# Two value stretches of eight heads instead of four of four, in the second layer's attention of a one-core kernel

## The reference

```python
qh = (q @ Wq).reshape(B, N, 16, 64).transpose(0, 2, 1, 3)
kh = (kv @ Wk).reshape(B, M, 16, 64).transpose(0, 2, 1, 3)
vh = (kv @ Wv).reshape(B, M, 16, 64).transpose(0, 2, 1, 3)
attn = softmax(einsum('bhnd,bhmd->bhnm', qh, kh) / 8)
out = einsum('bhnm,bhmd->bhnd', attn, vh)      # the "attention values"
x = x + tanh(g) * (out.reshape(B, N, 1024) @ Wo + bo)
# then layernorm, router (top 8 of 64), a shared expert, and the routed experts
```

## Time and profile before

| what | value |
|---|---|
| time, median of 3 runs | 2510.68 us (2510.32 to 2510.93) |
| span of the profiled execution | 2514.6 us |
| PE busy | 2403.0 us (96%) |
| PEld busy | 1805.6 us (72%) |
| ACT busy | 1612.6 us (64%) |
| DVE busy | 1597.9 us (64%) |
| POOL busy | 731.2 us (29%) |

### The profile page before, as it was taken

How to read it: one execution, slowest core, us unless ns; L and a number is a source line. 1 busy time by engine, 2 the same in 40 slices (tenths; PEclk the granted TensorE clock), 3 DMA queues, 4 the chain that set the end, 5 groups by cost and what they waited for, 6 DMA issues and landing times. The chain is left out here.

```text
span 2514.6 us, 63718 instructions
## 1 busy us (share of the span) xinstructions
PE 2403.0 (96%) x19932; PEld 1805.6 (72%) x19933; DVE 1597.9 (64%) x5004; ACT 1612.6 (64%) x4909; POOL 731.2 (29%) x871
## 2 busy tenths in 40 slices
PE   7999999999998899999999999999999967999997
PEld 5777777777777566666666666666666657888885
DVE  4777777777774466676776776776776753433338
ACT  3777777777774466666666666666666626777770
POOL 2000000000000022232233232233233245777771
PEclk7999999999999999999999999999999989999998
DMA  5111111111110501111111111111111257666679
GB/s 158 34 48 46 39 47 46 39 47 46 39 42 13 158 28 39 39 43 40 38 42 41 37 42 40 38 43 42 36 42 43 59 151 242 198 192 192 194 261 379
DMA packets 145291, 210.10 MB, mean 84 GB/s; under 512 B 23976, under 2 KB 108506, under 8 KB 145026
## 3 DMA queue, kind: packets, MB, share of 16 engines
q1 hardware_dynamic: 114322, 139.92, 19.0%
q0 software_dynamic: 26544, 60.21, 7.2%
q10 hardware_dynamic: 4160, 6.55, 0.7%
HBM read 118.21 MB, written 96.75 MB: 85 GB/s over the span
## 5 line engine op out<-in xcount | busy, mean ns | idle before, releaser
L1455 ACT ACTIVATE wup<-bank,nmax 112x375 f32<-112x375 f32 x512 | 297.2, 586 | 111.9 <-DVE nmax L1559 110.7
L767 ACT ACTIVATE prob<-bank,nmax 112x375 f32<-112x375 f32 x512 | 294.1, 587 | 54.9 <-DVE nmax L851 51.0
L851 DVE TENSOR_REDUCE nmax<-bank 112x1 f32<-112x375 f32 x512 | 254.9, 540 | 88.7 <-PE bank L589 88.7
L1903 POOL DMA_INDIRECT expert_rows<-rows,ids x248 | 237.2, 957 | 154.4 <-ACT wup L1455 107.3
L1559 DVE TENSOR_REDUCE nmax<-bank 112x1 f32<-112x375 f32 x512 | 255.5, 541 | 21.1 <-PE bank L1251 21.1
L1314 PE MATMUL bank<-wup,wk 128*128 128x375 f32 x512 | 219.9, 512 | 1.9 <-DMA wup<-context_turned 0.8
L1020 POOL TENSOR_TENSOR stats<-stats,neg_half 112x1 f32<-112x1 f32 x64 | 35.1, 549 | 632.3 <-DVE stats L881 628.3
L1461 ACT COPY pT<-bank 128x336 f32<-128x336 f32 x512 | 201.5, 451 | 19.3 <-PE bank L1258 19.1
L596 PE MATMUL bank<-ident,prob 112*128 112x112 f32 x1536 | 200.0, 263 | 7.6 <-ACT pT L773 1.7
L1870 POOL TENSOR_TENSOR stats<-stats,neg_half 112x1 f32<-112x1 f32 x64 | 35.6, 557 | 566.2 <-DVE stats L1590 564.0
L1251 PE MATMUL bank<-wup 64*112 64x375 f32 x1024 | 195.9, 501 | 3.3 <-ACT wup L1455 3.3
(11 more groups left out here) (284 smaller groups left out, 5321.4 us busy)
## 6 DMA issues: line engine op xcount, KB each, us to landing
xr<-expert_rows SPq DMA_DIRECT2D x274, 129.0 KB
wup<-expert_results SPq DMA_DIRECT2D x14, 1024.0 KB, 18.2
wdn<-expert_results SPq DMA_DIRECT2D x14, 1024.0 KB, 20.8
wdn<-in_L_ffn_W_down_dram SPq DMA_DIRECT2D x8, 1024.0 KB, 12.6
expert_rows<-nowhere SPq DMA_DIRECT2D x56, 129.0 KB, 2.9
x_and_h_in<-stage SPq DMA_DIRECT2D x32, 224.0 KB, 2.4
xt<-x_and_h_in SPq DMA_DIRECT2D x32, 224.0 KB, 2.8
context_turned<-ctxT SPq DMA_DIRECT2D x32, 187.5 KB, 2.2
```

Source lines behind the costliest of these rows:

```text
L767: nc.scalar.activation(prob[:, n % RING, :NK], s_bank[r][:NQ, :NK], ACT.Exp, bias=nmax[:, r:r + 1], accum_out=rsum[:, par, h:h + 1]).then_ ...
L851: nc.vector.tensor_reduce(nmax[:, r:r + 1], s_bank[r][:NQ, :NK], AX, ALU.max, negate=True).then_inc(maxed, 1)
L1455: nc.scalar.activation(prob[:, n % RING, :NK], s_bank[r][:NQ, :NK], ACT.Exp, bias=nmax[:, r:r + 1], accum_out=rsum[:, par, n:n + 1]).then_ ...
L1903: nc.gpsimd.indirect_dma_start(rows_d, bass.IndirectOffsetOnAxis(ap=ids[:, k:k + 1], axis=0), rows[:, k, :], None).then_inc(scattered, 16)
```

## The change

The values of a sequence are made in two stretches of eight heads (va0, va1) instead of four of four. Each of them now stands directly behind a group's scores on PE. The inverted sums follow: two reciprocals, two widened copies of 8 x 64 columns, two groups of four transposes, two copies to `rT`, two normalising multiplications, each over twice the columns. The ring of turned probabilities has 12 places instead of 8. `rexp`, `rT` and `xT` are laid into the space of a weight buffer that is free in this stage (`wup`), `x1ln` into a bias tile, and tanh works in place. The copy of lnT goes from DVE to ACT. The order list is laid anew: v11, lnT move to the act lane, k4 and k7 to the dve lane, and most slots change.

```diff
 ORDER_C = [
-    (1, "post", "va3", "dve"), (1, "own", "v10", "act"), (1, "own", "v11", "dve"),
-    (2, "own", "r0", "act"), (2, "post", "wo", "dve"), (3, "own", "v12", "act"), (3, "pre", "k2", "dve"),
-    (5, "pre", "k4", "act"), (5, "post", "lnT", "dve"), (6, "pre", "k1", "act"), (6, "pre", "xT", "dve"),
-    (7, "own", "va0", "dve"), (8, "pre", "k0", "act"), (8, "post", "router", "dve"), (9, "post", "shared_up", "act"),
-    (9, "pre", "k3", "dve"), (9, "own", "r1", "act"), (10, "pre", "k5", "act"), (10, "own", "va1", "dve"),
-    (10, "own", "r2", "act"), (12, "pre", "q0", "act"), (12, "pre", "v00", "dve"), (12, "pre", "v01", "act"),
-    (13, "post", "rank", "dve"), (13, "own", "r3", "act"), (14, "post", "shared_down", "dve"),
-    (14, "pre", "v02", "act"), (15, "pre", "k6", "dve"), (15, "pre", "q1", "act"), (15, "own", "va2", "dve"),
-    (15, "pre", "k7", "act"),
+    (1, "post", "va1", "dve"), (1, "own", "v10", "act"), (2, "own", "v11", "act"), (2, "post", "wo", "dve"),
+    (3, "own", "v12", "act"), (5, "pre", "k2", "dve"), (5, "post", "lnT", "act"), (6, "pre", "k4", "dve"),
+    (6, "pre", "k1", "act"), (6, "pre", "xT", "dve"), (7, "own", "r0", "act"), (7, "post", "router", "dve"), (7, "pre", "k0", "act"),
+    (8, "pre", "k3", "dve"), (8, "post", "shared_up", "act"),
+    (9, "own", "va0", "dve"), (9, "pre", "q0", "act"), (10, "pre", "k5", "act"), (11, "pre", "v00", "dve"),
+    (12, "pre", "v01", "act"), (13, "post", "rank", "dve"), (13, "pre", "v02", "act"), (14, "post", "shared_down", "dve"),
+    (14, "pre", "q1", "act"), (15, "pre", "k6", "dve"), (15, "own", "r1", "act"), (15, "pre", "k7", "dve"),
 ]
...
-    PT_RING = 8
+    PT_RING = 12
+    NG = 2
+    PER = H // NG
...
-                        freed(pe, i, later(*(f"v{g // 2}{c}" for c in range(KC))))
-                        wait_kept(pe, i, 4 * g + 4)
-                        for a in range(2):
+                        all_freed(pe, i, *(f"v{g}{c}" for c in range(KC)))
+                        wait_kept(pe, i, PER * (g + 1))
+                        for a in range(PER // 2):
...
                 def router(p, par, n):
                     misc = lane("router", n)
+                    other_lane("router", p, "lnT")
...
+                def keep_lnT(p, par, n):
+                    misc = full(act, "act", n)
+                    nc.scalar.copy(flat(x1T[:]), misc[:, :CC * NQ]).then_inc(lane_free["act"], 1)
...
-                    dve.wait_ge(exped, H * i + 4 * g + 4)
+                    dve.wait_ge(exped, H * i + PER * (g + 1))
...
-                    nc.vector.tensor_copy(rexp[:, g % 2, :].rearrange("q (h d) -> q h d", d=DK),
-                                          rinv[:, heads].unsqueeze(2).to_broadcast([NQ, 4, DK])).then_inc(expanded, 1)
+                    nc.vector.tensor_copy(rexp.rearrange("q (h d) -> q h d", d=DK),
+                                          rinv[:, heads].unsqueeze(2).to_broadcast([NQ, PER, DK])).then_inc(expanded, 1)
...
                 def inverses(i, par, n):
-                    for v, at in enumerate((0, 7, 8, 12)):
+                    for v, at in enumerate((4, 12)):
                         if n == at:
                             inverse(i, par, v)
...
-                sp.wait_ge(lane_full["dve"], uses.out(NB - 1, "va3"))
+                freed(sp, NB - 1, "va1")
                 experts_up(3)
```

More of the change, by code:

```diff
@@ L1091, in later @@
         return max(names, key=place)
-    for one, other in ([("xT", "q0"), ("xT", "q1"), ("va3", "wo"), ("wo", "lnT"), ("lnT", "router"), ("lnT", "shared_up"),
-                        ("router", "rank"), ("shared_up", "shared_down"), ("va0", "va1"), ("va1", "va2"), ("r0", "r1"), ("r1", "r2")]):
+    for one, other in ([("xT", "q0"), ("xT", "q1"), ("va1", "wo"), ("wo", "lnT"), ("lnT", "router"), ("lnT", "shared_up"),
+                        ("router", "rank"), ("shared_up", "shared_down"), ("r0", "va0")]):
         assert place(one) < place(other)
@@ L1331, in f @@
                         misc = lane(f"r{g}", n)
-                        pe.wait_ge(expanded, NT * p + g + 1)
-                        for a in range(2):
-                            mm = pe.transpose(misc[:, a * NQ:(a + 1) * NQ], rexp[:, g % 2, a * P:(a + 1) * P], ident[:NQ, :NQ])
+                        pe.wait_ge(expanded, NG * p + g + 1)
+                        for a in range(PER // 2):
+                            mm = pe.transpose(misc[:, a * NQ:(a + 1) * NQ], rexp[:, a * P:(a + 1) * P], ident[:NQ, :NQ])
                         left(mm, f"r{g}")
@@ L1374, in _ @@
                 hooks |= {f"q{g}": q(g) for g in range(2)} | {f"k{p}": k(p) for p in range(PAIRS)}
-                hooks |= {f"v{half}{c}": v(half, c) for half in range(2) for c in range(KC)} | {f"r{g}": inverse(g) for g in range(NT)}
-                hooks |= {f"va{g}": values(g) for g in range(NT)}
+                hooks |= {f"v{half}{c}": v(half, c) for half in range(2) for c in range(KC)} | {f"r{g}": inverse(g) for g in range(NG)}
+                hooks |= {f"va{g}": values(g) for g in range(NG)}
                 for _ in range(20):
@@ L1439, in room_in_pT @@
             def room_in_pT(eng, i, n):
-                g = n // 4 - PT_RING // 4
-                valued(eng, i if g >= 0 else i - 1, g % NT)
+                last = H * i + n - PT_RING
+                valued(eng, last // H, last % H // PER)
             def room_in_vals(eng, j, half):
-                valued(eng, j - 1, 2 * half + 1)
+                valued(eng, j - 1, half)
             @block.scalar
@@ L1452, in exponentials @@
                     if n == 0:
-                        wait(act, inverted, NT * (i - 1))
+                        wait(act, inverted, NG * (i - 1))
                     wait(act, turned, H * i + n + 1 - RING)
@@ L1460, in keep_turned @@
                     room_in_pT(act, i, n)
-                    nc.scalar.copy(pT[:, n % PT_RING, :], pt_bank[n % 2][:, :KC * NQ]).then_inc(kept_act, 1)
+                    nc.scalar.copy(pT[:, (H * i + n) % PT_RING, :], pt_bank[n % 2][:, :KC * NQ]).then_inc(kept_act, 1)
                 def q(g):
@@ L1488, in f @@
                         misc = full(act, "act", n)
-                        freed(act, p if g >= 2 else p - 1, f"va{(g - 2) % NT}")
-                        nc.scalar.copy(rT[:, g % 2, :], misc[:, :2 * NQ]).then_inc(lane_free["act"], 1)
-                    return f
+                        freed(act, p if g else p - 1, f"va{1 - g}")
+                        nc.scalar.copy(rT[:], misc[:, :PER // 2 * NQ]).then_inc(lane_free["act"], 1)
+                    return f
+                def keep_lnT(p, par, n):
+                    misc = full(act, "act", n)
+                    nc.scalar.copy(flat(x1T[:]), misc[:, :CC * NQ]).then_inc(lane_free["act"], 1)
                 def tanh_h(j):
@@ L1496, in tanh_h @@
                     wait(act, x2_ready, j)
-                    nc.scalar.activation(h_out[:], h_in[:], ACT.Tanh).then_inc(h_ready, 1)
+                    nc.scalar.activation(h_in[:], h_in[:], ACT.Tanh).then_inc(h_ready, 1)
                 def sigmoid_exp(p):
@@ L1511, in _ @@
                 hooks = {f"q{g}": q(g) for g in range(2)} | {f"k{p}": k(p) for p in range(PAIRS) if uses.lane[f"k{p}"] == "act"}
-                hooks |= {f"v{half}{c}": v(half, c) for half in range(2) for c in range(KC) if uses.lane[f"v{half}{c}"] == "act"} | {f"r{g}": inverse(g) for g in range(NT)}
-                hooks |= {"router": lambda p, par, n: sigmoid_exp(p), "shared_up": shared_exps}
+                hooks |= {f"v{half}{c}": v(half, c) for half in range(2) for c in range(KC) if uses.lane[f"v{half}{c}"] == "act"} | {f"r{g}": inverse(g) for g in range(NG)}
+                hooks |= {"router": lambda p, par, n: sigmoid_exp(p), "shared_up": shared_exps, "lnT": keep_lnT}
                 tanh_h(0)
@@ L1605, in moments_x @@
                     dve.wait_ge(h_ready, j + 1)
-                    nc.vector.scalar_tensor_tensor(out=src, in0=h_out[:], scalar=g_tanh[:NQ, 2:3], in1=src,
+                    nc.vector.scalar_tensor_tensor(out=src, in0=h_in[:], scalar=g_tanh[:NQ, 2:3], in1=src,
                                                    op0=ALU.mult, op1=ALU.add).then_inc(x2_ready, 1)
@@ L1735, in keep_x3 @@
                                                    in1=stage[:], op0=ALU.mult, op1=ALU.add).then_inc(lane_free["dve"], 1)
-                hooks = {"xT": keep_xT, "wo": residual, "lnT": keep_lnT,
+                hooks = {"xT": keep_xT, "wo": residual,
                          "router": keep_affinity, "rank": place_in, "shared_down": keep_x3}
@@ L1740, in _ @@
                 hooks |= {f"v{half}{c}": keep_v(half, c) for half in range(2) for c in range(KC) if uses.lane[f"v{half}{c}"] == "dve"}
-                hooks |= {f"va{g}": normalise(g) for g in range(NT)}
+                hooks |= {f"va{g}": normalise(g) for g in range(NG)}
                 parts_x = [(0, h_sum), (1, moments_x), (1, norm_x)]
@@ L1937, in _ @@
```

(2 more changed lines are left out.)

31 lines of the change are left out of this document (14 added, 17 removed).

## The result

The changed kernel took 2614.3 us (median of 4 runs, 2611.5 to 2615.9) against 2510.8 for the kernel before beside it (2510.3 to 2511.8): ratio 1.0412, 95% interval 1.0397 to 1.0426, or 103.5 us more, where 64 were forecast. The profiled execution spans 2613.5 us, 98.9 more than that of before. Of these 88.7 lie between the first and the last scores of layer 1's attention, 3.1 ahead of them, 5.0 from the last scores to the first matmul of the experts, and 2.1 in the experts.

A forecast was written before the change was run, and what follows sets the result against it. PE was taken as the bound, busy 37.56 of 37.57 us per sequence. Gain -1.04, lane waits +1.2 and the wait for rank +1.9 gave +2.06, over 31 repeats +64: 2575 us, range over the cases 2508 to 2602.

The forecast's parts named there:

- the gain: On PE: two value stretches fewer 0.66, one more neighbour to scores 0.18, wo's wait 0.2; together 1.04 us per sequence.
- the 0.18 for a return to the full shape: On PE: a key matmul between values and scores takes 0.83 us, between other full-array work 0.65.
- rank, DVE's order and POOL: shared_down on PE waits for rank's copy on DVE, behind the widened copy and weigh: 1.9 us with POOL's row copy.
- the two orders that were costed: POOL's row copy ahead of DVE's widened copy: PE waits 2.05 us; DVE first, weigh caught: about 1.7.
- Without POOL 0.43: PE's wait ahead of shared_down from DVE's own order alone: rank leaves at V + 5.58, PE is there at V + 5.15.
- the lanes: PE waits where a bank is used again before its copy is done: 1.2 us per sequence, bounds 0.9 and 1.8.
- others: v11's copy for q0, k5 and DVE work ahead of the maxima at n = 4: 0 to 0.4 us, taken as 0.1.
- The sum: -1.04 + 1.2 + 1.9 = +2.06 us per sequence, over 31 repeats +64 us.
- The shape: Rival: each of five changes of array shape saved on PE is worth 0.54 us; -1.3 per sequence, 2471 us; chance 0.14.
- clear of DVE: Rival: POOL's row copy misses DVE's steps because scatters land later; +0.6 us per sequence, 2529 us; chance 0.22.

The follow-up runs named there:

- list_late: list_only with POOL's row copy held until the twenty-first exponential; 2483.0 us, ratio 0.9890 to the kernel before.
- relaid_late: relaid with POOL's row copy held until the eighteenth exponential of a sequence; 2479.3 us, ratio 0.9872 to the kernel before.
- apart: list_only with key product k6 moved from behind wo to between a scores group and value stretch va1; 2514.5 us in one execution.
- late_fill: The changed kernel with POOL's row copy held until the eighteenth exponential counted from the start of a sequence; 2568.0 us.
- before_late: The kernel before with POOL's row copy held until the twentieth exponential; 2510.2 us, ratio 0.9990 to the kernel before.
- list_only: The changed kernel with stretches, ring and buffers kept and only the order list laid anew; 2498.4 us, ratio 0.9943 to the kernel before.
- dve_order: The changed kernel with DVE's steps moved: sigmoids before v00's copy, second inverse to slot 14, weigh behind rank's copy; 2552.2 us.
- relaid: The changed kernel with a further order list and other slots for DVE's parts; 2507.1 us, ratio 0.9981 to the kernel before.

## Why the prediction was right in kind and short by 40 us

**Right: the gain.** PE's own saving was put at 1.04 us per sequence. With the waits of the next paragraphs what is left for it is 37.57 + 2.2 + 1.9 - 40.6 = 1.1; that is a remainder, but list_late, where PE has no gap, gives the same 1.11 (36.46), and relaid_late 1.30. A stretch of 48 records takes 2.47 (2.45 forecast), and the 0.18 for a return to the full shape between scores and values is confirmed by apart (0.20). The Trainium skill, "TensorEngine Tiling (Array Packing)", section "Key Properties", says that a change of the tiling mode drains the array; apart agrees that leaving the mode and coming back has a price, 0.20 us here.

**Right: rank, DVE's order and POOL.** 1.9 us were forecast ahead of shared_down and 1.90 measured, behind the releaser named, in 26 sequences; POOL came first, one of the two orders that were costed. Without POOL 0.43 was forecast, and late_fill leaves 0.31: the turned heads ahead of shared_down take 0.89 there instead of 0.58. before_late shows the part of the argument that had only been reasoned: the same collision in front of an idle stretch is free. The Trainium skill, "SBUF — State Buffer", section "Who interferes with whom", adds to the copies that the prediction named those DVE steps that have two inputs in SBUF while POOL reads SBUF, and says that a reduction never contends. The runs agree on the first: 1.79 against 0.27 for the silu's product. On the second they agree as far as they go, 1.46 for three maxima either way, but these read a PSUM bank.

**Mis-sized: the lanes, "Together 0.22 + 0.10 + 0.36 + 0.44 + 0.1, 1.2; bounds 0.9 and 1.8".** Start against start, by the sequence shown, with what each neighbour takes where nothing holds it up:

| wait on PE | forecast | measured |
|---|---|---|
| v11 behind v10's copy | 0.22 | 0.26 |
| xT behind k4's copy | 0.10 | 0.24 |
| k7 behind k6's copy | 0.36 | 0.42 |
| k0 behind r0's copy | 0.44 | 0.53 |
| others: k5 0.22, k0 and k3 0.16, shared_up 0.11, wo 0.10, k5's edge 0.09, turned heads 0.08 | 0.10 | 0.76 |
| sum | 1.2 | 2.2 |

The four waits that were worked out came out 0.04 to 0.14 too low each; hand-over had been taken as nothing, which would fit, but was not measured by itself. Most of the miss is the line of others: k5 for q0's copy, which was seen and called even, and the act lane behind k0, where one late copy makes the next use late as well, which was not followed. The 1.0 by which the lanes were missed is the whole difference between the 2.06 forecast and the 3.0 measured (40.6 less 37.6), over 31 sequences some 30 us. The entries of about 0.1 depend by some hundredths on the undisturbed row with which they are compared.

**Left out: the end.** The sum took 31 times the sequence and nothing else. The last interval from wo to wo takes 31.2 us instead of 25.8, 5.4 more. Columns as in the earlier trace rows, the changed kernel's interval with its stretch at the lower clock, then the interval of the kernel before:

```profile
2101.44:2132.63 31.19, 24.06 (x198) 18.78 (x196) 16.28 (x59) 14.19 (x44) 14.65 (x18) 0.84 0.29 84
...
2120.90:2131.00 10.10, 7.53 (x52) 6.55 (x54) 5.45 (x28) 2.31 (x6) 5.14 (x7) 0.50 0.41 114
```

```profile
2009.70:2035.52 25.82, 20.72 (x195) 15.52 (x195) 17.57 (x65) 14.23 (x45) 10.95 (x15) 1.00 0.20 58
```

The changed kernel's PE at the start of that stretch:

```profile
2120.82 1.38 PE L1259 MATMUL bank<-ident,wup 112*128 112x112 f32 x6 [2.20 <-ACT pT L1463]
```

PE is busy for 24.06 us instead of 20.72, 3.3 of the 5.4: from 2120.9 to 2131.0 it was granted 0.50 of its clock, the lower of its two levels (1.2 instead of 2.4 GHz), right behind a wait of 2.20 for ACT's copy of turned probabilities. The other 2.0 are more waiting. All versions with two stretches show it, 27.6 to 31.9 us for this interval at a granted clock of 0.83 to 0.94, while the kernel before and before_late have 25.8 at 1.00: relaid_late gained 1.30 in each of 30 sequences, 39 us, lost 5.7 in the last, and gained 33 in the time.

From the first wo to the last the profiled execution is 95.8 us longer than that of before, 32 more than forecast: 29 in the 30 regular intervals, 3 in the last. The other 8 of the 103.5 can't be placed by one trace per version. Stages whose code is the same vary by as much (over all versions the first scores begin at 832.1 to 840.3 us, and the experts take 435.1 to 438.7), so the 3.1 ahead of the scores and the 2.1 in the experts are not shown to be the change's; and the profiled execution of before was itself a long one, its span 3.9 above its median.

**Not foreseen: the clock in four sequences.** In the four intervals of 42.2 us, q1 behind shared_down takes 2.8 to 3.0 us from start to start instead of 1.77, and no releaser is named. It is the granted clock. From shared_down's start to k6's, one of the four first, then the regular sequence shown above:

```profile
1112.97:1117.48 4.51, 4.51 (x24) 4.44 (x25) 2.61 (x16) 2.04 (x7) 0.00 (x0) 0.62 0.27 75
1356.60:1359.46 2.86, 2.86 (x24) 2.79 (x25) 2.60 (x16) 1.70 (x6) 0.00 (x0) 1.00 0.07 21
```

The same 24 records take 1.65 us longer at a granted clock of 0.62. In all four PE had just stood still for 1.9 us ahead of shared_down, and no other version, none of which has that gap, shows a clock below 1.00 between its second wo and its last but one. Why it fell behind this gap in four sequences and not in the other 22 is open.

**Refuted rivals.** The shape is not worth 0.54 per change (apart); POOL was not clear of DVE (26 of 32 sequences). Rival B, that the new stretches, ring or buffers cost by themselves, fell with list_only.

**Open.** What makes the 0.1 by which list_late beat its expectation was not separated.

## What to carry to other kernels

A list that gains on the bound engine is worth no more than the slack it leaves on the lanes: work out every reuse of a bank (start of the matmul to end of the copy against what PE has to do in between), follow a late one to the next use of that lane, and put a term for those not worked out that is as large as those that were. When an engine that is off the critical path runs a long copy, ask which steps of its neighbour on DVE it falls on: moving DVE's steps changed which one was hit, to one that PE does not wait for (dve_order, 2.0 us per sequence gained, part of it by the order itself) or to one that it does (relaid, 0.4 lost). One wait that put POOL's copy where DVE idles, or has only steps that PE hardly waits for, gave 0.4 to 1.4 us per sequence, wherever PE had been waiting for the step that was hit. And look at the granted clock of a stretch that takes longer without a releaser.

## What the runs showed of the hardware

Beside POOL's 1.89 us row copy (SBUF to SBUF), some of DVE's steps ended 0.1 to 0.3 us behind it, however short they are elsewhere: a widening copy 2.01 instead of 0.43, a SCALAR_TENSOR_TENSOR on 64 columns 1.29 instead of 0.22, a TENSOR_TENSOR on 112 columns 1.79 instead of 0.27. Others beside the same copy were not slowed: a RECIPROCAL on 64 columns, also from SBUF to SBUF (0.55 in list_only), and steps that read a PSUM bank, such as the reductions (three in 1.46) and rank's copy (0.21). POOL's copy itself took 1.89 in each of these.

TensorE's granted clock was 1.00 from the second wo to the last but one in every version, except behind four of the changed kernel's 26 gaps of 1.9 us (0.62 over the 4.51 us shown). In the last interval of the changed kernel it was 0.50 for 10.1 us, behind a wait of 2.20.
